# Causal mask from half-row products, maxima written into the stacked queries, and a new table of turns

## What is computed

```python
# _L0_attn_ref (k=0); x here is the normalized one
q = split_heads(x @ Wq + bq)          # 16 heads of 16 columns; k, v likewise
attn = jnp.einsum('bhqd,bhkd->bhqk', q, k) / jnp.sqrt(jnp.float32(D))
alibi = slopes[:, None, None] * (jnp.arange(T, dtype=jnp.float32) - (T - 1))[None, None, :]
attn = attn + alibi
causal = jnp.tril(jnp.ones((T, T), dtype=bool))[None, None]
attn = jnp.where(causal, attn, jnp.finfo(jnp.float32).min)
p = jax.nn.softmax(attn, axis=-1)
o = jnp.einsum('bhqk,bhkd->bhqd', p, v).transpose(0, 2, 1, 3).reshape(B, T, C)
return o @ Wo + bo
# _L3_attn_ref (k=3): q, k = rope(q), rope(k); 16 heads of 16 columns, no mask
attn = jax.nn.softmax(scores, axis=-1)
# the whole
x = x + _L0_attn_ref(xn, ...) + _L0_ffn_ref(xn, ...)   # ternary weights, 256 -> 1024 -> 256
x = x + _L1_attn_ref(xn, ...) + _L1_ffn_ref(xn, ...)   # convolution, gated recurrence, group norms; 16 experts
x = x + _L2_attn_ref(xn, ...) + _L2_ffn_ref(xn, ...)   # one head of 256 columns; spline-made weights
x = x + _L3_attn_ref(xn, ...) + _L3_ffn_ref(xn, ...)   # rope; 8 experts mixed by top-2 weights
```

## Time and profile before

| | before |
|---|---|
| median of 3 runs | 1648.97 us |
| profiled execution, own time | 1639.4 us |
| its span | 1638.1 us |
| busy of the span: TensorE, weight loads, VectorE, ScalarE, GpSimd | 1399.5, 821.9, 1005.6, 654.0, 411.3 us |
| first stage, 80 to 505 us: TensorE, VectorE, ScalarE busy | 394.5, 250.2, 182.4 us |
| last stage, 1138 to 1638 us: TensorE, VectorE, ScalarE busy | 426.3, 296.0, 207.2 us |
| granted TensorE clock in those stages | 0.90, 0.88 |

### The profile page before, as it was taken

The page is one execution under the profiler, slowest core; times in us unless marked ns, Lnnn a source line. Parts: engine busy times, 40 slices in busy tenths (PEclk is TensorE's granted clock), DMA queues, the critical chain, the costliest instruction groups (busy, mean ns, idle before and its releaser), DMA issues.

```text
span 1638.1 us, 18683 instructions
## 1 busy us (share of the span) xinstructions
PE 1399.5 (85%) x7204; PEld 821.9 (50%) x7204; DVE 1005.6 (61%) x1854; ACT 654.0 (40%) x930; POOL 411.3 (25%) x399
## 2 busy tenths in 40 slices
PE   1588989989999877699758999999789889889886
PEld 0355655656566544355326767766335335335333
DVE  6875575555555898876388353357775765655651
ACT  3333453444545653256113242230353453352352
POOL 2443141231211142121274132142213302302300
PEclk9969999899889987799759999999699988889989
DMA  7000000000023000016333000003101000100100
GB/s 221 7 1 1 1 1 1 1 1 1 20 62 139 10 26 26 1 49 184 115 98 32 1 1 0 1 9 74 38 0 35 19 1 1 52 1 1 52 1 13
DMA packets 32009, 53.10 MB, mean 32 GB/s; under 512 B 5456, under 2 KB 19760, under 8 KB 31280
## 3 DMA queue, kind: packets, MB, share of 16 engines
q1 hardware_dynamic: 27840, 40.99, 8.1%
q0 software_dynamic: 4080, 10.92, 3.1%
HBM read 43.89 MB, written 10.52 MB: 33 GB/s over the span
## 4 chain that ended last, share of the span: by engine, by line
PE 42%; DVE 15%; ACT 4%; issue 3%; POOL 2%; DMA 1%; SPq 0%; DVEq 0%; POOLq 0%
PE pair L610 17%; PE bank L610 14%; DVE max L1088 4%; PE bank L686 3%; ACT probs L1577 2%; PE pair L673 2%; POOL gathered L1932 1%; PE pair L643 1%; PE pair L653 1%; DMA gathered<-outbox,slots 1%; DVE qs L1104 1%; DVE mix_h L1496 1%; PE pair L664 1%; DVE conv L1177 1%; DVE normed L1248 0%
## 5 line engine op out<-in xcount | busy, mean ns | idle before, releaser
L1088 DVE TENSOR_REDUCE max<-pair 128x2 f32<-128x1024 f32 (+3 forms) x256 | 251.5, 1017 | 116.6 <-PE pair L656 64.0
L1577 ACT ACTIVATE probs<-pair 128x1024 f32<-128x1024 f32 (+3 forms) x256 | 209.8, 867 | 203.0 <-PE pair L676 123.8
L1890 POOL TENSOR_TENSOR h_low<-hidden,h_high 128x512 fp32r<-128x512 f32 x64 | 82.4, 1294 | 278.0 <-ACT h_high L1612 277.8
L673 PE MATMUL pair<-qs,ks 52*128 52x512 f32 (+3 forms) x512 | 116.6, 479 | 26.4 <-DVE max L1088 13.4
L653 PE MATMUL pair<-ks,qs 50*128 50x512 f32 (+3 forms) x512 | 121.7, 486 | 20.2 <-DVE max L1088 16.0
L686 PE MATMUL bank<-probs,v 128*32 128x512 f32 (+3 forms) x1024 | 130.8, 587 | 3.9 <-ACT probs L1577 3.1
L610 PE MATMUL pair<-wqk,xnT 128*128 128x512 f32 x192 | 101.4, 654 | 14.4 <-DVE cut_low L1026 10.8
L673 PEld LDWEIGHTS pair<-qs,ks 52*128 52x128 f32 x512 | 50.0, 203 | 122.8 <-issue 40.1
L1129 DVE TENSOR_TENSOR x<-bank,x 128x512 f32<-128x512 f32 x32 | 22.0, 688 | 119.4 <-PE bank L610 119.4
L653 PEld LDWEIGHTS pair<-ks,qs 50*128 50x128 f32 x512 | 52.7, 205 | 77.5 <-DVE max L1088 33.1
L1950 POOL TENSOR_TENSOR h<-mix_h,h 128x512 bf16<-128x512 f32 x48 | 55.3, 1165 | 128.5 <-DVE mix_h L1496 102.1
(11 more groups left out here) (295 smaller groups left out, 2856.0 us busy)
## 6 DMA issues: line engine op xcount, KB each, us to landing
expert_in<-in_experts_in SPq DMA_DIRECT2D x16, 352.0 KB, 4.3
expert_out<-in_experts_out SPq DMA_DIRECT2D x16, 256.0 KB, 4.8
h<-comb SPq DMA_DIRECT2D x4, 1024.0 KB, 5.3
x<-in_x SPq DMA_DIRECT2D x4, 512.0 KB, 10.3
wqk<-in_wqk SPq DMA_DIRECT2D x4, 512.0 KB, 3.6
tern_raw<-in_ffn_in SPq DMA_DIRECT2D x8, 256.0 KB, 6.8
inbox<-zeros SPq DMA_DIRECT2D x4, 512.0 KB, 5.4
tokens<-inbox SPq DMA_DIRECT2D x16, 128.0 KB, 2.2
```

Source lines behind the costliest of these rows:

```text
L673: made = mm(to[:, hh, q0:T], m.ks[g % 2][r0:r0 + AUG + 4, p, kt * P:(kt + 1) * P], m.qs[g % 2][r0:r0 + AUG + 4, p, q0:T], start=True, stop ...
L1088: V.tensor_reduce(m.max[:, g % 2, p, qt, :], to[:, :, 0:n], AX.X, ALU.max).then_inc(*s.done("top"))
L1577: A.activation(m.probs[(2 * kt + p) % 4][:, :, q0:T], to[:, :, q0:T], ACT.Exp).then_inc(*s.done("exp"))
L1890: Q.tensor_tensor(m.h_low[k][:, j, :], m.hidden[k][j % 2][:, :], m.h_high[k][:, j, :].bitcast(F32), ALU.subtract).then_inc(*s.done("low"))
```

## The change

Four things are done together.

1. **Mask by half rows** (`masked`). For each `score` and `prob` of k=0, four matmuls take the place of two. Each contracts over the 64 rows of its head's half (rows 0 to 63 or 64 to 127), and writes 64 of the diagonal block's 128 columns: the stationary operand is now a 64 x 128 part of the mask, the moving one a 64 x 64 identity. The masks are laid out for that (`by_halves`), and `mask_kq` moves to another address. The list of TensorE then has 1024 mask matmuls where it had 512, and as many weight loads.
2. **Maxima through the stack.** `shift` writes minus the maximum into columns 50 and 51 of each head's queries in `stack`. `refold` turns the query half of the stack a second time (8 fp32r turns, where `lift` had 8 plain fp32 turns), and ScalarE copies the result over the whole of `qs` (`refolded`), where VectorE added it (`lifted`). `max_cols` is gone. `cut` of group g+2 now waits for `refold` of group g, not for its `fold`.
3. **The loads** of `gates1` and `rest1` wait for the last `refold` of k=0 where they waited for the last `fold`.
4. **Turns dealt out anew.** All of `DUE` changes, on every engine. In the first stage the 8 `unit`s of a sequence now stand between the `qkv`s of a sequence, for two sequences at its start and for two in its middle, and the `down`s behind them; most groups in between have only their own parts. Before, most groups had a `unit` or a `down` among them.

```diff
@@ DUE @@
-    "lift": "33 61 94 116 145 176 209 231 260 291 324 351 377 403 430 454 754 ...
+    "refold": "47 48 91 120 144 168 195 219 279 280 323 351 375 399 426 450 757 ...
-    "unit": "16 17 30 31 52 53 57 59 89 90 141 142 165 166 171 172 204 205 256 257 ...
+    "unit": "14 15 17 18 20 21 23 24 55 56 58 59 61 62 64 65 238 239 241 242 244 245 ...
...
+    def masked(blocks, mask):
+
+        for part in PAIRS:
+            for hh in PAIRS:
+                rows_ = slice(STACK * hh, STACK * hh + STACK)
+                made = mm(blocks[:, hh, part * STACK:(part + 1) * STACK], mask[rows_, part, :], m.ident16[rows_, :], start=False, stop=part == 1)
+        return made
...
     def score(k, b, g, p, qt):
...
         if k == 0:
-            for hh in PAIRS:
-                made = mm(to[:, hh, n - P:n], m.ident16[:, :], m.mask_qk[:, :], start=False, stop=True)
+            made = masked(to[:, :, n - P:n], m.mask_qk)
...
-    def lift(k, b, g):
-        to = bank("lift", k, b, g)
+    def refold(k, b, g):
+
+        to = bank("refold", k, b, g)
         pe.wait_ge(*at("shift", k, b, g))
-        for p in PAIRS:
-            for qt in range(TT):
-                made = turn(to[:, p, qt * P:(qt + 1) * P], m.max_cols[:, p, qt, :, :].rearrange("p h r -> p (h r)"), m.ident)
-        made.then_inc(*s.done("lift"))
+        for tt in range(TT):
+            for p in PAIRS:
+                made = turn(to[:, p, tt * P:(tt + 1) * P].bitcast(F32R), m.stack[g % 2][:, tt, 0, 2 * p:2 * p + 2, :].rearrange("p h r -> p (h r)"), m.ident_r[:, :])
+        made.then_inc(*s.done("refold"))
...
     def prob(k, b, g, kt, p):
         to = bank("prob", k, b, g, kt, p)
-        pe.wait_ge(*at("lifted", k, b, g))
+        pe.wait_ge(*at("refolded", k, b, g))
...
     def cut(k, b, g):
...
-            dve.wait_ge(*at("fold", k, b2, g2, 0))
             dve.wait_ge(*at("fold", k, b2, g2, 1))
+            dve.wait_ge(*at("refold", k, b2, g2))
...
     def shift(k, b, g):
         dve.wait_ge(*s.last("top", [(k, b, g, p, qt) for p in PAIRS for qt in range(TT)]))
-        dve.wait_ge(*at("set_pool", k))
-        if 4 * b + g >= 1:
-            b2, g2 = (b, g - 1) if g >= 1 else (b - 1, G - 1)
-            dve.wait_ge(*at("lift", k, b2, g2))
-        top_, cols = m.max[:, g % 2, :, :, :].rearrange("p a t h -> p (a t h)"), m.max_cols[:, :, :, :, :].rearrange("p a t h r -> p (a t h) r")
-        V.tensor_scalar(cols[:, :, AUG + 2].bitcast(F32R), top_, -1.0, None, ALU.mult).then_inc(*dve.up())
-        dve.wait_ge(*dve.own())
-        V.scalar_tensor_tensor(cols[:, :, AUG + 3], top_, -1.0, cols[:, :, AUG + 2], ALU.mult, ALU.subtract).then_inc(*s.done("shift"))
-
-    def lifted(k, b, g):
-        to, qs = bank("lift", k, b, g), m.qs[g % 2]
-        dve.wait_ge(*at("lift", k, b, g))
-        V.tensor_tensor(qs[:, :, :], to[:, :, :], qs[:, :, :].bitcast(F32), ALU.add).then_inc(*s.done("lifted"))
+        dve.wait_ge(*at("fold", k, b, g, 0))
+        top_, cols = m.max[:, g % 2, :, :], m.stack[g % 2][:, :, 0, :, AUG + 2:AUG + 4]
+        V.tensor_scalar(cols[:, :, :, 0], top_, -1.0, None, ALU.mult).then_inc(*dve.up())
+        dve.wait_ge(*dve.own())
+        V.scalar_tensor_tensor(cols[:, :, :, 1], top_, -1.0, cols[:, :, :, 0].bitcast(F32), ALU.mult, ALU.subtract).then_inc(*s.done("shift"))
...
+    def refolded(k, b, g):
+        to = bank("refold", k, b, g)
+        act.wait_ge(*at("refold", k, b, g))
+        A.copy(m.qs[g % 2][:, :, :], to[:, :, :]).then_inc(*s.done("refolded"))
...
+def by_halves(a):
+
+    halves = a.astype(np.float32).reshape(2, STACK, P).transpose(1, 0, 2)
+    return np.concatenate([halves, halves])
...
-            "mask_qk": above.astype(np.float32), "mask_kq": np.ascontiguousarray(above.T, dtype=np.float32),
+            "halves": np.concatenate([ident[0:STACK, 0:STACK]] * 2), "mask_qk": by_halves(above.T), "mask_kq": by_halves(above),
```

More of the change, by code:

```diff
@@ L55 @@
         "turn": keys(ALL, B), "qkv": keys(HEADS, B, range(TT)), "fold": keys(HEADS, B, range(G), PAIRS),
-        "score": keys(HEADS, B, range(G), PAIRS, range(TT)), "lift": keys(HEADS, B, range(G)),
+        "score": keys(HEADS, B, range(G), PAIRS, range(TT)), "refold": keys(HEADS, B, range(G)),
         "prob": keys(HEADS, B, range(G), range(TT), PAIRS), "weigh": keys(HEADS, B, range(G), range(TT)),
@@ L71 @@
         "cut": keys(HEADS, B, range(G)), "top": keys(HEADS, B, range(G), PAIRS, range(TT)), "shift": keys(HEADS, B, range(G)),
[L72 removed]
+        "headed": keys(HEADS, B, range(G)), "joined": keys(ALL, B, PAIRS),
         "gated": keys((0, 2), B, range(UNITS)), "mean_out": keys(B), "fed": keys(B, PAIRS),
@@ L301 @@
 PLACES = {"pair": ((0, 1), (2, 3), (4, 5)), "acc": ((6,),), "one": ((7,),), "two": ((6,), (7,))}
-BANKS = {"tern_sum": "pair", "turn": "pair", "qkv": "pair", "fold": "pair", "score": "pair", "lift": "pair", "prob": "pair", "weigh": "acc", "back": "one",
+BANKS = {"tern_sum": "pair", "turn": "pair", "qkv": "pair", "fold": "pair", "score": "pair", "refold": "pair", "prob": "pair", "weigh": "acc", "back": "one",
          "rows": "pair", "unit": "pair", "down": "one", "mean": "one", "proj": "pair", "gate": "two", "gamma": "pair", "inflow_turn": "pair", "mem_turn": "two",
@@ L321 @@
     "score": lambda k, b, g, p, qt: [("top", (k, b, g, p, qt))],
-    "lift": lambda k, b, g: [("lifted", (k, b, g))],
+    "refold": lambda k, b, g: [("refolded", (k, b, g))],
     "prob": lambda k, b, g, kt, p: [("exp", (k, b, g, kt, p))],
@@ L674, in prob @@
         if k == 0:
-            for hh in PAIRS:
-                made = mm(to[:, hh, q0:q0 + P], m.ident16[:, :], m.mask_kq[:, :], start=False, stop=True)
+            made = masked(to[:, :, q0:q0 + P], m.mask_kq)
         made.then_inc(*s.done("prob"))
@@ L681, in weigh @@
         pe.wait_ge(*at("v_out", k, b, kt))
-        pe.wait_ge(*at("exp", k, b, g, kt, 0))
-        pe.wait_ge(*at("exp", k, b, g, kt, 1))
+        for p in PAIRS:
+            pe.wait_ge(*at("exp", k, b, g, kt, p))
         q0 = kt * P if k == 0 else 0
@@ L928, in mix @@
         made.then_inc(*s.done("mix"))
-    parts = {"tern_sum": tern_sum, "turn": turn_x, "qkv": qkv, "fold": fold, "score": score, "lift": lift, "prob": prob, "weigh": weigh, "back": back, "rows": rows, "out": out,
+    parts = {"tern_sum": tern_sum, "turn": turn_x, "qkv": qkv, "fold": fold, "score": score, "refold": refold, "prob": prob, "weigh": weigh, "back": back, "rows": rows, "out": out,
              "unit": unit, "down": down, "mean": mean, "proj": proj, "gate": gate, "gamma": gamma, "inflow_turn": inflow_turn, "mem_turn": mem_turn, "shared": shared,
@@ L1825, in cast0 @@
     def cast0():
-        for name, tile_ in (("groups", m.groups), ("ident", m.ident16), ("mask_qk", m.mask_qk), ("mask_kq", m.mask_kq), ("earlier", m.earlier)):
-            Q.dma_start(tile_[:, :], d[name]).then_inc(*s.cast_landing())
+        for name, tile_ in (("groups", m.groups), ("halves", m.ident16), ("mask_qk", m.mask_qk), ("mask_kq", m.mask_kq), ("earlier", m.earlier)):
+            Q.dma_start(tile_[tuple([slice(None)] * len(tile_.shape))], d[name]).then_inc(*s.cast_landing())
     def set_pool(k):
@@ L2014, in load @@
         elif name == "gates1":
-            sp.wait_ge(*s.last("fold", [(0, BATCH - 1, g, half) for g in range(G) for half in PAIRS]))
+            sp.wait_ge(*s.last("refold", [(0, BATCH - 1, g) for g in range(G)]))
             send(m.wgates[:, :, :], d["wgates1"], landing)
```

17 lines of the change are left out of this document (7 added, 10 removed), and 282 rows, old and new, of the table DUE.

## The result

The changed kernel takes 1567.35 us (median of 4 runs, 1562.3 to 1571.69) where the kernel before took 1647.13 in the same comparison. Repeated later with six runs it was 0.951 (0.947 to 0.955). The profiled execution has 1562.3 us, its span 1561.0.

What follows compares the result with a forecast made beforehand. TensorE, busy 85% of the span, was taken to bound the kernel; the terms -29 - 9 - 8 - 7 - 8 + 16 + 5 gave -40 us, a median of 1609 us, range 1574 to 1655 (the forecast's own 1590 to 1630).

Steps and rivals of the forecast that it cites:

- Masks: Masked rounds of k=0: half-row masks cut a round from 0.56 to 0.45 us in 256 rounds, -29 us.
- the exposed score load stays (0.20), then the stream (0.15), then one exposed mask load: Masked rounds of k=0: the make-up of the expected 0.45 us a round, the mask load taken at 0.10.
- New turns: Both attention stages: -7 start of attention, -8 head of last stage, +16 attention without filler, +5 clock.
- 10.8 us, I leave as they are: First stage: TensorE's waits for the ternary feed-forward's input were expected unchanged, bounds 0 to -7 us.
- hid the latency: First stage: without filler, 13 bare groups get three waits of 0.4 us each, +16 us, bounds 0 and +31.
- New maxima: Second query turn in fp32r, -9 us, and ScalarE's copy replacing VectorE's addition, -8 us.
- Start of attention: First folds of k=0: units between the `qkv`s give work beside the cuts, against waits of 3.39 and 3.22, -7 us.
- Head of the last stage: Start of k=3: the 4.96 us wait for mix_comb goes and some 3 us of maxima lie beside outs, -8 us.
- The first rival: Bare stretches of the first stage: clock stays low throughout, +72 in place of +5, 1676 us; chance 0.11.
- that mask pairs cost what they cost today: Masked rounds of k=0: each of two mask pairs costs today's 0.22, +56 in place of -29, 1694 us; chance 0.06.
- all loads hide: Masked rounds of k=0: -90 in place of -29, half given back by other engines' latencies, 1578 us; chance 0.13.
- That time between 505 and 1138 us moves by no more than 5 us: Between 505 and 1138 us: nothing expected though turns are dealt anew; moving more than 5 us would prove the forecast wrong.

Runs made afterwards that it cites:

- M: Only the half-row masks, put into the kernel before with its old turns and maxima: 1591.55 us, ratio 0.970.
- T: Only the turns dealt out anew, in the kernel before with full-row masks and old maxima, `lifted` in its better places: 1608.38 us, ratio 0.977.
- X: The new maxima through the stack; added last to half-row masks and new turns they complete the changed kernel: 1567.35 us, ratio 0.951.
- T with M: Half-row masks and new turns but the old maxima, `lifted` up to two places later, against the kernel before: 1588.51 us, ratio 0.961.
- all but M: The changed kernel with its new turns and maxima, but the old full-row masks: 1571.06 us, ratio 0.956 to the kernel before.
- masks twice: The changed kernel with its four mask matmuls done twice in each round: 1555.33 us, ratio 0.946 to the kernel before; repeated, 1549.15 us, 0.942.

## Why the prediction was wrong

The direction was right and that each round would be shorter; the sum was half of what came. Two terms failed, the price of a masked round and the turns. With the parts in the order M, T, X the ratios are 0.970, 0.961 and 0.951: 49, 16 and 16 us. The medians are 1591.55, 1588.51 and 1567.35. The first two intervals overlap (0.964 to 0.977 and 0.953 to 0.968), so what T adds to M is not clear of noise; T and X together add 24 to 31 us to M, where 11 were forecast.

- **Masks, forecast -29, measured -49 alone (-54 by the medians).** The step that failed is "the exposed score load stays (0.20), then the stream (0.15), then one exposed mask load", 0.45 us a round in the mean. It measured 0.38: 0.18 less in each round, 47 us. Some 9 us more are clock, which I hadn't counted here, less 5 us of longer waits. At 512 columns the round is 0.41 and not 0.55: 0.32 to 0.34 for the score's pair, 0.07 for all four masks. The 0.20 itself was misread. I took the earlier trace rows for a pair of 0.43 and one of 0.23, but they are 0.34 and 0.32 (rows below the list); the 0.43 is what a pair costs with full-row masks on both sides. A pair between half-row masks takes 0.32 (205.43 to 205.75), so 0.1 went of the 0.20, which I had left as it was.
- **New turns, forecast +6 (-7 - 8 + 16 + 5), measured -38 without the masks, and -3 (medians) to -16 (ratios) with them.** The steps that failed are the waits for the feed-forward input, "10.8 us, I leave as they are", and the product of a unit or down of which I counted only that it "hid the latency". The 10.8 us went; with M alone, in the old turns, 10.2 are still there. The added waits for probs and maxima of the bare stretches are real, 12.5 us against 4.1, half of the 16 forecast. I had valued filler by what it hides and never what it waits for: with full-row masks the bare stretches wait 3.6 us in all, where the kernel before waited 27.
- **New maxima, forecast -17, measured -16 to -21.** Right in size. The turn takes 0.81 and not 0.70, and the rest is VectorE's: it lies in the last stage, where waits fall from some 67 us in T with M to 50. That stage's list also had 9.3 us of probs waiting for maxima, which the 24.7 of the prediction leave out; they didn't shrink (11.3).
- **Start of attention, -7:** wrong in its place; the folds wait 3.50 and 2.32 where they waited 3.39 and 3.22. **Head of the last stage, -8:** its mix_comb wait went and its maxima grew from 10.18 to 14.71; from the end of k=0 on, T with M is no faster than before (1126 against 1122 us).
- **The parts don't add.** M 49 and all but M 73 make 122; both bring 80. My sum treated them as independent. Each alone ends a good part of the same half-speed stretches (33 us lost before, 18 with M, 19 with T). With all three the rounds save 42 us more work than with full-row masks, of which waits and half clock take all but 8 in the first stage. The first rival (the clock stays low in bare stretches) is therefore partly right: not all 13 groups, but above all one stretch of 30 us, which costs at most 15 us. It runs at full clock with masks twice and with the masks in the other order.
- **The rivals:** that mask pairs cost what they cost today, or that all loads hide, is excluded by the pitches (0.18 saved a round, against -0.22 and 0.35). That time between 505 and 1138 us moves by no more than 5 us was right as far as it can be read: from the last mask of k=0 to the first product with the spline weights of k=2 it was 341 us and is 345; behind it work of k=3 has moved ahead of that of k=2.

The second pair of the earlier trace rows starts at 1546.81 (kernel before):

```profile
1546.81 0.39 PE L673 MATMUL pair<-qs,ks 52*128 52x512 f32 x2
```

Three pairs in a row, between full-row matmuls, take 0.91 us (1215.27 to 1216.18), so a pair between two others takes some 0.23 to 0.25, and the first and the last some 0.1 more:

```profile
1215.27 0.74 PE L673 MATMUL pair<-qs,ks 52*128 52x512 f32 x4
1215.85 0.40 PE L653 MATMUL pair<-ks,qs 50*128 50x512 f32 x2
1216.18 1.06 PE L686 MATMUL bank<-probs,v 128*32 128x512 f32 x8
```

The loads of the new masks (timeline of the weight loads, changed kernel), to be held against the earlier trace rows:

```profile
205.36 0.12 PEld L650 LDWEIGHTS pair<-ident,mask_kq 64*128 64x128 bf16 x4 [0.15 <-issue]
```

The rule of the Trainium skill (TensorE: Matmul & The Clock Gate, LDWEIGHTS) that a load's time goes by columns agrees with these rows, 0.12 us for four half-row loads of 128 columns against 0.11 for two whole ones, if two halves load at once, which is what TensorEngine Tiling (Array Packing), Key Properties, of the Trainium skill states. That this is the reason isn't shown: with two masks of the same half one behind the other the masks' part was 0.07 as well. The change of tiling mode that drains the engine, in the same section, fits a part: a pair took 0.43 next to full-row masks and 0.32 between half-row ones. No run tells what the 0.09 are that are left over 0.23. Its overhead of about 60 cycles for each matmul (Instruction Overhead) would be an estimated 25 ns at 2.4 GHz. Four masks take 0.07 us together and eight 0.13, under 18 ns each: too little for one after another, but no contradiction if two run side by side.

## What to carry to other kernels

Where TensorE's clock goes between two levels, price a change in three columns: work at full clock, waits, and microseconds lost to half clock, stretch by stretch; here the second and third took back most of the 42 us that the masks saved in the new turns. Read what an instruction costs at half clock from rows at half clock: a masked round took 1.6 times (before) and 1.8 times (after) as long there, not twice. Before valuing a removed filler by what it covers, list what it itself waits for. An instruction on an in-order engine that waits for another engine is worth as much as its place: moving one sum up to two places was worth about as much as replacing it (22 and 21 us by the medians).

## Not expected of the hardware

A kernel with 1024 needless matmuls more is 1.0% faster than the changed one (1549.15 against 1565.17 us, all runs apart) and the fastest of all here. The fall of the clock at 230 us comes back at the same place in both profiles of the changed kernel, at waits of no more than 0.3 us, and stays away with the same work and nearly the same waits when the four masks stand in another order. Three pairs of half-row products of 512 columns take 0.91 us and two take 0.66: the first and the last cost some 0.1 more than one between. Four matmuls of 64 columns with their loads, in the half rows that the matmuls before them use, add 0.07 us between two rounds, and 0.16 ahead of a weigh.
